# Weighted sums of an attention kernel in groups of eight key tiles in place of four, with eleven probability buffers in place of seven

## The reference

```python
x = x + conv3x3(group_norm(x), weight)            # x: (8, 64, 56, 56)
t = to_tokens(x)                                  # (8, 3136, 64)
n = layer_norm(t)
q, k, v = n @ Wq.T + bq, n @ Wk.T + bk, n @ Wv.T + bv
t = t + softmax(q @ k.T / 8) @ v                  # one head of 64, over all 3136 tokens of an image
n = layer_norm(t)
p = softmax(n @ gate_w + gate_b); top 2 of 16 experts, their p renormalised
t = t + sum over the two experts of p_e * ((silu(n @ w1[e]) * (n @ w2[e])) @ w3[e])
x = from_tokens(t)
```

## Time and profile before

| | |
|---|---|
| median of 3 runs | 2696.83 us (2693.95 to 2698.46) |
| the profiled execution | 2697.52 us |
| its span, from the first to the last instruction | 2695.8 us |
| mean granted clock of TensorE | 0.963 |
| PE busy | 2443.3 us (91%), 13821 matmuls |
| DVE busy | 1804.3 us (67%) |
| ACT busy | 1298.4 us (48%) |
| POOL busy | 1012.8 us (38%) |
| weighted sum (L1475), PE | 2800 records, 622.1 us |
| reductions for the maxima (L1116), DVE | 1400, 845.1 us |

### The profile page before, as it was taken

How to read it: one execution, slowest core, us unless ns; L and a number is a source line. 1 busy time by engine, 2 the same in 40 slices (tenths; PEclk the granted TensorE clock), 3 DMA queues, 4 the chain that set the end, 5 groups by cost and what they waited for, 6 DMA issues and landing times.

```text
span 2695.8 us, 46824 instructions
## 1 busy us (share of the span) xinstructions
PE 2443.3 (91%) x13821; PEld 1635.1 (61%) x13821; DVE 1804.3 (67%) x5891; ACT 1298.4 (48%) x2986; POOL 1012.8 (38%) x1097
## 2 busy tenths in 40 slices
PE   5899989999999999999999999999999999997773
PEld 3455555566666666666666666666666666664662
DVE  5576676667776777677766776677767777774432
ACT  2344444455554555455555555455555555453542
POOL 2022005300344424442444324443344324465765
PEclk8899999999999999999999999999999999997875
DMA  3143101111112222222222122222222112222442
GB/s 75 27 92 78 43 21 46 47 41 39 52 50 62 48 58 62 59 55 53 57 57 62 48 51 68 56 54 54 54 54 55 45 42 59 55 54 65 122 95 51
DMA packets 226560, 152.98 MB, mean 57 GB/s; under 512 B 100240, under 2 KB 216720, under 8 KB 226320
## 3 DMA queue, kind: packets, MB, share of 16 engines
q1 hardware_dynamic: 190880, 98.26, 14.0%
q0 software_dynamic: 31456, 48.03, 7.5%
q10 hardware_dynamic: 3984, 3.70, 0.5%
HBM read 83.92 MB, written 65.27 MB: 55 GB/s over the span
## 4 chain that ended last, share of the span: by engine, by line
PE 62%; DVE 17%; issue 5%; POOL 2%; ACT 1%; DMA 0%; POOLq 0%; ACTq 0%; DVEq 0%
PE ps_o L1475 17%; PE ps_m L1435 8%; PE ps_s L1463 7%; PE ps_s L1464 6%; DVE max_part L1116 5%; PE ps_z L1501 4%; PE ps_z L1648 3%; PE ps_x L1634 3%; PE ps_z L1623 2%; PE ps_s L1634 1%; PE ps_y L1538 1%; PE ps_y L1554 1%; DVE v_s L1029 1%; PE ps_y L1449 1%; PE ps_y L1562 1%
## 5 line engine op out<-in xcount | busy, mean ns | idle before, releaser
L1116 DVE TENSOR_REDUCE max_part<-ps_m 128x1 f32<-128x448 f32 x1400 | 845.1, 620 | 607.4 <-PE ps_m L1435 595.2
L951 ACT ACTIVATE prob<-ps_s 128x448 f32<-128x448 f32 x1400 | 758.7, 545 | 579.2 <-PE ps_s L1464 549.8
L1475 PE MATMUL ps_o<-prob,v_s 128*64 128x448 f32 x2800 | 622.1, 552 | 0.0
L1435 PE MATMUL ps_m<-k_a,q_a 128*128 128x448 f32 (+3 forms) x1600 | 540.1, 365 | 64.5 <-DVE max_part L1116 55.3
L1463 PE MATMUL ps_s<-q_a,k_a 128*128 128x448 f32 x1400 | 586.5, 419 | 2.4 <-ACT prob L951 0.8
L780 POOL DMA_INDIRECT got<-sorted_y,slot x448 | 425.6, 950 | 423.5 <-PE ps_s L1464 219.5
L759 POOL DMA_INDIRECT sorted_x<-xn,slot x448 | 426.3, 952 | 324.8 <-PE ps_s L1464 168.8
L1464 PE MATMUL ps_s<-q_b,k_a 128*128 128x448 f32 x1400 | 512.0, 366 | 0.0
L1435 PEld LDWEIGHTS ps_m<-k_a,q_a 128*128 128x128 f32 (+1 forms) x1600 | 294.7, 188 | 162.8 <-DVE max_part L1116 131.5
L1475 PEld LDWEIGHTS ps_o<-prob,v_s 128*64 128x64 f32 x2800 | 178.7, 136 | 274.1 <-issue 250.7
L1463 PEld LDWEIGHTS ps_s<-q_a,k_a 128*128 128x128 f32 x1400 | 265.3, 189 | 107.8 <-issue 84.6
(11 more groups left out here) (186 smaller groups left out, 2971.1 us busy)
## 6 DMA issues: line engine op xcount, KB each, us to landing
fx<-sorted_x SPq DMA_DIRECT2D x43, 384.0 KB
sorted_y<-fy SPq DMA_DIRECT2D x42, 320.0 KB
xh<-in_x SPq DMA_DIRECT2D x96, 126.0 KB
fx<-sorted_x SPq DMA_DIRECT2D x47, 256.0 KB
sorted_x<-fy POOLq DMA_DIRECT2D x28, 320.0 KB, 6.0
sorted_x<-xn,slot POOLq DMA_INDIRECT x448
got<-sorted_y,slot POOLq DMA_INDIRECT x448
x_now<-in_x SPq DMA_DIRECT2D x112, 56.0 KB
```

The costliest lines, as they stand in the source:

```text
L951: a.activation(prob[(at.n * KEY_TILES + i) % PROBS][:], ps_s[(at.n * KEY_TILES + i) % 2][:, 0:CHUNK], ACT.Exp).then_inc(s["p_ready"], 1)
L1116: v.tensor_reduce(max_part[n % 2][0:here.stop - here.start, j, kb:kb + 1], ps_m[(passes_before(n) + m) % 2][0:here.stop - here.start, 0:CH ...
L1435: done = t.matmul(ps_m[before % 2][0:here.stop - here.start, first:last], q_a[:].rearrange("p a c -> p (a c)")[:, here], keys, start=True, ...
L1475: t.matmul(ps_o[side:side + CHANNELS, 0:CHUNK], v_s[u % 2][:, i, :], prob[(n * KEY_TILES + i) % PROBS][:], start=(i < 2), stop=(i >= KEY_T ...
```

## The change

Three things follow from two constants. The weighted sum runs in groups of eight tiles at steps 9 (tiles 0 to 7) and 17 (tiles 8 to 15); LAST_GROUP becomes 16, so nine tiles (16 to 24) are weighed at step 1 of the next body. Eleven buffers hold exponentials, since tile 16 is read only at that step.

```diff
 MAX_TO, MAX_TO_FEW = 22, 21
 ASK_AT = 8
-GROUP = 4
+GROUP = 8
 Z_AFTER = 2
-PROBS = 7
+PROBS = 11
 KEY_TILES = -(-TOKENS // 128)
```

## The result

| | median us | runs |
|---|---|---|
| before | 2696.07 | 2693.95 to 2698.46 |
| changed | 2721.27 | 2719.78 to 2721.83 |

What follows compares the result with a forecast made beforehand. PE was taken to set the time, with DVE right behind it from step 9 to step 20. Chunk terms +11.8, +8.8, -4.9, -1.2 and -7.6 summed to +6.9 us: 2703.7 at the median, own range 2694 to 2714, wider 2680 to 2724.

Steps and rivals of the forecast that it cites:

- The sign and its reason: Whole kernel: slower, since the group at step 13 is exchanged for tiles at step 17 at 0.67 to 1.50 us.
- The stretch 13 to 16: Ordinary middle chunk, steps 13 to 16: shorter, but between 4.9 and 5.4 us and not 4.0.
- A: Whole kernel: PE alone counts and edges are won in full, 56 chunks at -0.67 us, 2660 us; chance 0.15 with its half.
- rival B: Step 21: DVE's lateness cuts the saving; 0.6 us in 33 middle chunks gives +20 us, 2724 us; chance 0.17.
- signs of being wrong: Stretch 13 to 16 falling over 1.2 us, step 21 falling less than 1.4 us, or the clock falling in the middle.
- the chances: Whole kernel against the kernel before: slower 0.48, within 0.30, faster 0.22; what can be told from no change is 5.4 us.
- Step 5, 9 and 1: Ordinary middle chunk: group removed at step 5 -1.45 us, four tiles added at step 9 +1.40, at step 1 +1.50.
- Steps 13 and 17: Ordinary middle chunk: removal at step 13 gives only DVE's wait, -0.67 us; four more tiles at step 17 cost +1.50.
- Step 21: Ordinary middle chunk: removing the group saves the full 1.86 us, just fitting DVE's wait of 1.85 us.
- The last image: Seven chunks without convolution, normalisation or keys to prepare: PE's own sum with three full removals, -1.08 us a chunk.
- First and fourth chunks, and the first eleven: First of an image (routing) +1.75 us, fourth (expert codes) -0.98, the eleven without expert work -0.11, each per chunk.

Runs made afterwards that it cites:

- the best version: Kernel before with selected chunks' groups moved from step 5 to 9 and 21 to 1, and sum ahead of maximum at 17 or 21; 2645.16 us against 2700.82.

## Why the prediction was right, and where it was off

**The sign and its reason** were right. The stretch 13 to 16 of the ordinary chunk came out at 4.94 us, inside the 4.9 to 5.4 named; PE waits for hid at step 15 and for its bank at step 17, as said; the single run of this exchange costs 41 us. The rival that wins all edges (A, 2660) is excluded: at step 13 only half came off. The rule of the Trainium skill, "TensorEngine Tiling (Array Packing)", Key Properties, that changing the tiling mode drains TensorE holds as far as it goes (PE's busy time fell by 31 us), but says nothing on who waits.

**The size** was not right. 2721.3 us lies outside the forecast's own range, 2694 to 2714. It lies near rival B's 2724, but this is chance: waits of B's kind brought some 5 us and not 20, as shown below. Of the signs of being wrong that the prediction named, two came in part: step 21 fell by less than 1.4 us in the third chunk of an image and in three of the last image, and the clock fell in the middle. The group of eight took 3.23 us, about the 3.1 to 3.2 named. DVE waited 1.22 us behind the one of step 9 and 2.07 behind that of step 17 (1 to 1.5 named). Added up as the prediction says, the chances are 0.47, 0.32 and 0.21, and not 0.48, 0.30 and 0.22.

**Step 5, 9 and 1**: -1.50, +1.36 and +1.53, against -1.45, +1.40, +1.50.

**Steps 13 and 17**: -0.91 and +1.67, against -0.67 and +1.50, together +0.76 against +0.83. The division was off because the wait at step 17's maximum grew (0.17 in the earlier trace rows, 0.35 now) and lies in the second stretch.

**Step 21 (rival B's place)**: -1.74 in the second and sixth chunks, against -1.86, but -1.24 in the third and -1.53 in the fifth. I had read a chunk where the negated maximum comes at step 22 and PE needs it at step 23 (second, fourth, sixth and seventh of an image), and the first. In the third and fifth chunk, as in the first, it is due a step earlier, and PE runs into it. Changed kernel, chunk 30, DVE and then PE, steps 21 and 22:

```profile
1403.55 0.42 DVE L1291 TENSOR_TENSOR hid<-up,ps_x 128x256 f32<-128x256 f32 x1
1403.89 0.17 DVE L1124 TENSOR_REDUCE max_neg<-max_part 128x3 f32<-128x21 f32 x1
...
1404.11 0.74 PE L1449 MATMUL ps_y<-ident,max_neg 64*128 64x64 f32 x4 [0.52 <-DVE max_neg L1124]
```

The wait of 0.52 us was not there before. In the fifth chunk it is 0.2 us: the transposition starts 0.49 us behind the last maximum, where 0.29 was the distance before. PE's wait of 0.55 us for its bank after the combining, from which rival B had reasoned, is there before and after alike (0.55 and 0.53 us, chunk 32), so it took nothing away. So DVE does cut the gain at step 21, as B said, but at another place than B had it. Against the forecast 0.62 us are missing in the third chunk and 0.33 in the fifth, some 5 us in these eleven chunks.

**The last image** is the step that failed: -1.08 us a chunk was taken as PE's own sum with three full removals, without a row of that image, and +0.68 was measured, a difference of 10.6 us in six chunks, the largest of all. The removals at steps 5, 13 and 21 gave 0.70, 0.83 and 1.41 us in place of 1.86 each. At step 13 PE waits for hid, as in the other images, in five of the six chunks (0.7 to 1.0 us). At step 5 it is DVE's pace, since the convolution that DVE waited for is gone. Chunk 52, steps 5 to 8, before and changed:

```profile
2308.57:2314.19 5.62, 5.62 (x32) 3.90 (x31) 5.38 (x22) 3.06 (x7) 1.70 (x3) 1.00 0.14 41
```

```profile
2334.74:2340.27 5.53, 4.57 (x24) 3.26 (x23) 5.29 (x22) 3.18 (x7) 1.64 (x2) 1.00 0.14 42
```

DVE is busy for 5.38 of 5.62 us, so giving up the group brings 0.09 us. It brings 0.3 us or less in chunks 50 and 54 too, and 1.3 in the other three. The added tiles at step 9 cost 0.8 to 1.2 us in all of the six but chunk 52, where they cost 0.1. The first of these rows could have been read beforehand. I had argued that less work means that PE sets the time, but PE had lost more work there than DVE (8.68 to 5.62 us against 6.67 to 5.38, with chunk 26 for comparison).

**First and fourth chunks, and the first eleven**: +1.51, -0.87 and -0.09 against +1.75, -0.98 and -0.11. These sums came out close in part by luck. In the first eleven, step 9 cost 0.43 less than forecast and step 13 gave 0.20 less, and smaller differences fill the rest. In the fourth chunk, step 9 cost 0.22 less and step 17 0.51 more; one clock fall is in the latter.

**The sum.** Of the 15.9 us between forecast and measurement up to chunk 55, the last image is 10.6 and the ordinary chunks 5.8. In these, step 21 missed by 7.1 us, and the two seventh chunks in which the clock fell add some 3.4; a cheaper step 9 takes back about 4, and the rest is small. No term of the prediction stood for the clock.

## What to carry to other kernels

When two engines are level, work taken off one of them is worth only the wait that the other has in that stretch, while work added where the other idles costs in full. So move work towards a wait that exists. Read the length of that wait from the chain to the one result that is waited for, not from an engine's total, and read it anew for each kind of chunk. Where a matmul waits for its bank, the order of two pieces of work at that step is worth trying first: here it was worth 23 us and no buffer, though it lost 1.5 us at step 17 in each chunk of the last image, where DVE had much to do behind the delayed maximum.

## What the runs showed of the hardware

In four of the 56 groups of eight tiles at step 17 the changed kernel's weighing took 4.4 to 4.9 us and not 3.23. TensorE's granted clock falls to half there. Changed kernel, around chunk 27, step 17 (length, busy times, then the clock in the third last column), and the weight loads in it:

```profile
1248.00:1257.60 9.60, 6.94 (x45) 5.56 (x44) 7.26 (x29) 5.20 (x13) 5.61 (x7) 1.00 0.05 9
1257.60:1261.10 3.50, 3.50 (x11) 1.26 (x13) 2.90 (x16) 0.00 (x0) 1.73 (x2) 0.54 0.23 46
1261.10:1264.50 3.40, 3.40 (x21) 1.84 (x19) 0.00 (x0) 1.14 (x5) 0.00 (x0) 0.97 0.22 59
```

```profile
1259.38 0.24 PEld L1475 LDWEIGHTS ps_o<-prob,v_s 128*64 128x64 f32 x2 [0.51 <-issue]
1260.12 0.24 PEld L1475 LDWEIGHTS ps_o<-prob,v_s 128*64 128x64 f32 x2 [0.51 <-issue]
1261.46 0.14 PEld L1475 LDWEIGHTS ps_o<-prob,v_s 128*64 128x64 f32 x2 [0.35 <-issue]
1261.84 0.14 PEld L1475 LDWEIGHTS ps_o<-prob,v_s 128*64 128x64 f32 x2 [0.23 <-issue]
```

The half pairs of one group are 0.74 us apart at a clock of 0.5 (1.2 GHz) and 0.38 at full clock (2.4 GHz). Ahead of the fall PE had been busy for 6.94 of 9.60 us. The excess of the four groups is 5.8 us. The kernel with only step 13 given up has seven such groups and 10.3 us; the best version has none of eight tiles and 0.7 us in one of four.

The falls are tied to waits of PE. In every fall up to chunk 54, in all the traces, a wait of PE of 0.7 to 2.2 us had ended within 3 us ahead. Between 110 and 2400 us of the span PE waits for over 0.7 us 36 times before and 81 times in the changed kernel, and the clock falls once and five times; in the best version it waits so 20 times, and the clock falls once, in the last chunk. But a wait does not decide it. Chunk 20, step 17, before, and in the kernel with only step 5 given up (its lines are 13 further down):

```profile
939.76 0.48 PE L1435 MATMUL ps_m<-k_a,q_a 128*128 128x448 f32 x1 [1.69 <-DVE max_part L1116]
940.16 1.73 PE L1475 MATMUL ps_o<-prob,v_s 128*64 128x448 f32 x8
```

```profile
933.68 0.48 PE L1448 MATMUL ps_m<-k_a,q_a 128*128 128x448 f32 x1 [1.69 <-DVE max_part L1129]
934.09 2.98 PE L1488 MATMUL ps_o<-prob,v_s 128*64 128x448 f32 x8
```

The wait is the same 1.69 us and the group of four tiles the same; the clock is full in the first and 0.55 in the second. That kernel has four such groups, all of four tiles at step 17 and none of its groups of eight at step 9, so neither the long group nor the wait alone brings the fall. What else does is open, and that fewer waits would bring fewer falls was not tried by itself.
